# Value and query projections first, gate projections last, within each block of a fused retention and mixture-of-experts kernel

## What is computed

```python
xn = layernorm(x)                                  # no scale, no shift
q, v = xn @ Wq, xn @ Wv
states = scan(lambda prev, vt: lam * prev + vt, v) # along the tokens
y = q * states
y = (y - mean(y)) * rsqrt(var(y) + 1e-5) * ln_g + ln_b   # over 1024 features
attn = (y * silu(xn @ Wg)) @ Wo
# router: top 8 of 64 experts for a token, at most 128 tokens an expert
h  = silu(xg @ w1[e].T) * (xg @ v1[e].T)           # 384 wide
ffn = scatter_add(weight * (h @ w2[e]))
out = x + attn + ffn
```

## Time and profile before

| | |
|---|---|
| time, median of 3 runs | 2774.52 us (2772.79 to 2777.97) |
| the profiled execution: time / span | 2767.81 us / 2766.1 us |
| PE busy | 2572.7 us, 93% |
| DVE busy | 1640.1 us, 59% |
| ACT busy | 1295.2 us, 47% |
| POOL busy | 633.0 us, 23% |
| mean granted TensorE clock | 0.967 of full |

### The profile page before, as it was taken

One profiled execution on the slowest core, in us unless ns is written; L12 is line 12 of the kernel. 1 busy time (PEld: TensorE's weight loads), 2 busy tenths in 40 slices (PEclk: granted clock), 3 DMA queues, 4 the chain that ended last, 5 costly groups with the idle time before them and its releaser, 6 DMA issues.

```text
span 2766.1 us, 41220 instructions
## 1 busy us (share of the span) xinstructions
PE 2572.7 (93%) x13849; PEld 2280.4 (82%) x13849; DVE 1640.1 (59%) x1718; ACT 1295.2 (47%) x1474; POOL 633.0 (23%) x521
## 2 busy tenths in 40 slices
PE   4799699999999899998999989999899998999997
PEld 4787588879888798887988889888898888988786
DVE  7868745466545655547655575545755457554664
ACT  5533234445544455444644455444554445544454
POOL 1001212132221412113221241221321214221321
PEclk8899899999999999999999999999999999999998
DMA  7646375658855587656875569756686567956576
GB/s 279 220 151 212 122 231 162 223 171 257 263 189 191 183 270 236 212 172 201 273 253 188 175 208 296 233 162 209 221 264 227 180 204 221 294 174 213 184 246 162
DMA packets 147556, 590.16 MB, mean 213 GB/s; under 512 B 20096, under 2 KB 36544, under 8 KB 147008
## 3 DMA queue, kind: packets, MB, share of 16 engines
q1 hardware_dynamic: 112128, 503.71, 50.7%
q0 software_dynamic: 35392, 86.00, 15.5%
HBM read 520.89 MB, written 85.50 MB: 219 GB/s over the span
## 4 chain that ended last, share of the span: by engine, by line
PE 68%; DMA 12%; issue 9%; DVE 6%; ACT 3%; POOL 2%; POOLq 0%; ACTq 0%; DVEq 0%
PE psA L1165 15%; PE psA L1167 15%; PE psA L1166 14%; DMA out_dram<-ot 7%; DMA out_dram<-ys,s_idx 5%; PE psH L1165 5%; PE psH L1167 4%; PE psH L1166 4%; PE psY L1165 2%; PE psY L1167 2%; PE psY L1166 2%; DVE yb L960 2%; ACT ew_hi L632 1%; PE psX L1269 1%; DVE ew_lo L913 1%
## 5 line engine op out<-in xcount | busy, mean ns | idle before, releaser
L913 DVE TENSOR_TENSOR ew_lo<-ew_raw,ew_hi 128x1536 fp32r<-128x1536 f32 x377 | 667.3, 1778 | 395.5 <-ACT ew_hi L632 389.9
L632 ACT ACTIVATE ew_hi<-ew_raw 128x1536 fp32r<-128x1536 f32 x384 | 567.2, 1487 | 176.2 <-DMA ew_raw<-ew_dram 104.2
L1165 PE MATMUL psA<-xT_hi,pw_hi 128*128 128x512 f32 x1536 | 616.9, 402 | 2.0 <-DVE pw_lo L908 2.0
L1167 PE MATMUL psA<-xT_hi,pw_lo 128*128 128x512 f32 x1536 | 608.6, 396 | 0.0
L1166 PE MATMUL psA<-xT_lo,pw_hi 128*128 128x512 f32 x1536 | 604.2, 393 | 0.0
L626 ACT ACTIVATE pw_hi<-pw_raw 128x1024 fp32r<-128x1024 f32 x256 | 267.8, 1061 | 515.9 <-PE psA L1167 515.9
L908 DVE TENSOR_TENSOR pw_lo<-pw_raw,pw_hi 128x1024 fp32r<-128x1024 f32 x256 | 309.0, 1218 | 257.6 <-ACT pw_hi L626 252.2
L1165 PE MATMUL psH<-ew_hi,gT_hi 128*128 128x384 f32 x1024 | 360.3, 352 | 37.5 <-DVE gT_lo L934 37.5
L1166 PE MATMUL psH<-ew_lo,gT_hi 128*128 128x384 f32 x1024 | 354.2, 346 | 0.0
L1167 PE MATMUL psH<-ew_hi,gT_lo 128*128 128x384 f32 x1024 | 353.8, 346 | 0.0
L1167 PEld LDWEIGHTS psA<-xT_hi,pw_lo 128*128 128x128 f32 x1536 | 290.8, 189 | 69.9
(11 more groups left out here) (152 smaller groups left out, 3318.8 us busy)
## 6 DMA issues: line engine op xcount, KB each, us to landing
ew_raw<-ew_dram SPq DMA_DIRECT2D x384, 768.0 KB, 5.7
pw_raw<-proj_w_dram SPq DMA_DIRECT2D x256, 512.0 KB, 3.6
xn_scratch<-xt SPq DMA_DIRECT2D x33, 512.0 KB, 3.8
xt<-x_dram SPq DMA_DIRECT2D x32, 512.0 KB, 5.9
out_dram<-x_dram SPq DMA_DIRECT2D x32, 512.0 KB, 5.0
out_dram<-ot POOLq DMA_DIRECT2D x32, 512.0 KB, 13.6
xn<-xn_scratch SPq DMA_DIRECT2D x29, 512.0 KB, 6.2
xn_scratch<-wt SPq DMA_DIRECT2D x33, 32.0 KB, 1.5
```

The source lines that it names most:

```text
L632: act.activation(ew_hi[:, c % 3, :], ew_raw[:, c % 3, :], ACT.Copy).then_inc(s_ewhi, 1)
L913: dve.tensor_tensor(ew_lo[:, c % 3, :], ew_raw[:, c % 3, :], ew_hi[:, c % 3, :].bitcast(F32), ALU.subtract).then_inc(s_ewlo, 1)
L1165: pe.matmul(dst, l_hi, r_hi_, start=first, stop=False)
L1167: return pe.matmul(dst, l_lo, r_hi_, start=False, stop=last)
```

## The change

The order of the projections in a block changes. The loop becomes `vq`: four steps with four projections each (v, q, v, q). The eight gate projections follow it, straight in the code, and the part between is laid under them. `Wg` moves behind `Wv`, `Wq` in the table of weights, and the loads follow the new order. The number of matmuls is the same.

v always goes to bank 0 of `psA` and q to bank 1. Token sums and their transpose move to `psH`, the shifts to `psY`. The shift (now `shift_in`) and the gating (`gate_in`) go chunk by chunk, with a semaphore `s_t` of their own; a shift matmul waits until the shift two before has been added. POOL no longer makes the low part of expert piece 1. Its gather in the loop moves ahead of the second `add_sums`. In block 0 the 16 rounds are 3 a step and then 4 under the gates.

```diff
@@ vector engine, loop @@
                     scan(j, mm, 0)
                     S(2)
-                    find(0)
+                    next8(0)
                     times_q(j, mm, 0)
                     S(3)
-                    strike(0)
                     if with_e:
                         hT_lo_of(e)
                         piece_lo(e + 1, 0)
+                    next8(1)
+                    scan(j, mm, 1)
+                    if with_e:
+                        piece_lo(e + 1, 1)
+                        gT_lo_of(e + 1)
+                        piece_lo(e + 1, 2)
                     S(4)
-                    if with_e:
-                        piece_lo(e + 1, 1)
-                        piece_lo(e + 1, 2)
-                        gT_lo_of(e + 1)
-                    find(1)
-                    strike(1)
-                    scan(j, mm, 1)
+                    times_q(j, mm, 1)
                     S(5)
-                    find(2)
-                    times_q(j, mm, 1)
-                    S(6)
-                    strike(2)
-                    S(7)
-                    find(3)
-                    strike(3)
+                    next8(2)
                     if with_e:
                         hidden_part(e + 1)
@@ vector engine, under the gates @@
+                for m in range(2, KC):
+                    G(m + 2)
+                    if not with_e and m < 6:
+                        find8(keys[:, :], l1, 10 + m, s_ext, s_l1)
+                        strike8(keys[:, :], 10 + m, s_ext)
+                    if m == 2:
+                        shift_in(j, 0)
+                    shift_in(j, m - 1)
+                    if m == 2:
+                        gate_in(j, 0)
+                    if m == KC - 1:
+                        shift_in(j, m)
+                    gate_in(j, m - 1)
+                gate_in(j, KC - 1)
                 if with_e:
                     piece_lo(e + 1, 3)
-                z_of(j, 3)
@@ gpsimd @@
+                def vq(mm):
                     add_sums(j, mm, 0)
                     if with_e:
                         scatter(e0 + mm, 4 * j)
+                        gather_next(e0 + mm + 1)
                     add_sums(j, mm, 1)
-                    if with_e:
-                        gather_next(e0 + mm + 1)
...
-                    if with_e and m == 1:
-                        scatter(e0 + 4, 4 * j)
-                        gather_next(e0 + 5)
@@ scalar engine, under the gates @@
+                for m in range(2, KC):
+                    G(m + 2)
+                    gate(j, m)
+                    if m == 2:
+                        z_hi_of(j, 0)
+                    z_hi_of(j, m - 1)
                 if with_e:
                     piece_hi(e + 1, 3)
-                z_his(j, 2)
-                z_his(j, 3)
+                z_hi_of(j, KC - 1)
@@ tensor engine @@
-                token_sums(j)
+                g_proj(j, 0)
+                if with_e:
+                    hidden_turn(e)
+                token_sums(j)
+                g_proj(j, 1)
+                if with_e:
+                    output_mm(e)
+                    gather_turn(e + 1)
                 token_turn(j)
-                if with_e:
-                    gather_turn(e + 1)
-                shifts(j, 0)
-                if with_e:
-                    output_mm(e, (1,))
-                for i in range(1, 4):
-                    shifts(j, i)
-                    if with_e:
-                        hidden_mm(e + 1, (i - 1,))
-                if with_e:
-                    hidden_mm(e + 1, (3,))
+                g_proj(j, 2)
+                pe.wait_ge(s_t6, j + 1)
+                if with_e:
+                    pe.wait_ge(s_ys, e + 1)
+                shift(j, 0)
+                for m in range(3, KC):
+                    shift(j, m - 2)
+                    g_proj(j, m)
+                shift(j, KC - 2)
+                if with_e:
+                    hidden_mm(e + 1, (0,))
+                shift(j, KC - 1)
+                if with_e:
+                    hidden_mm(e + 1, (1, 2, 3))
```

More of the change, by code:

```diff
@@ L405, in run @@
                 with_e = e0 is not None
-                def qvg(mm):
+                def vq(mm):
                     per = NTOK // P // (KC // 2)
-                    for a in range(2, 8):
-                        if with_e and a == 6:
+                    for a in range(2, 6):
+                        if with_e and a == 4:
                             load_rest(e0 + mm + 1)
-                        load_proj(a % 2, 6 * mm + a + 2, n1(j, mm, a) + 1)
+                        load_proj(a % 2, 4 * mm + a + 2, n1(j, mm, a) + 1)
                         if not with_e:
-                            for i in range((a - 2) * per // 6, (a - 1) * per // 6):
+                            for i in range((a - 2) * per // 4, (a - 1) * per // 4):
                                 copy_x(per * mm + i)
@@ L417, in qvg @@
                         load_first(e0 + mm + 2)
-                each_qvg(sp, qvg)
+                each_vq(sp, vq)
+                for m in range(2, KC + 2):
+                    if with_e and m == 4:
+                        load_rest(e0 + 5)
+                    load_proj(m % 2, 2 * KC + m + 2, ng(j, m) + 1)
                 if with_e:
-                    load_rest(e0 + 5)
                     load_first(e0 + 6)
@@ L525, in run @@
                 if with_e:
[L526 to L530, removed]
+                    scatter(e0 + 4, 4 * j)
+                    gather_next(e0 + 5)
                 for m in range(KC - 1):
@@ L1065, in qvg @@
[L1065 to L1069 removed]
+                    S(4)
+                    times_q(j, mm, 1)
+                    S(5)
+                    next8(2)
                     if with_e:
                         hidden_part(e + 1)
[L1073 removed]
+                each_vq(dve, vq)
+                G = lambda m: proj_lo(ng(j, m), m % 2)
+                e = None if not with_e else e0 + 4
@@ L1098, in run @@
                 if with_e:
-                    hidden(e + 1)
                     piece_lo(e + 1, 4)
                     piece_lo(e + 1, 5)
-                if not with_e:
+                    hidden(e + 1)
+                else:
+                    dve.wait_ge(s_l1, SLOTS // 8)
+                    dve.tensor_copy(l2[:, 0:SLOTS], l1[0:SEL, :]).then_inc(s_lf, 1)
                     dve.wait_ge(s_l2, 16)
@@ L1317, in token_turn, with shift @@
                 for t in range(NT):
-                    o = pe.transpose(psA[:, 1, t * P:(t + 1) * P], tok6[:, t, :], ident[:, :])
+                    o = pe.transpose(psH[:, 1, t * P:(t + 1) * P], tok6[:, t, :], ident[:, :])
                 o.then_inc(s_tT, 1)
-            def shifts(j, i):
-                if i == 0:
-                    pe.wait_ge(s_t6, j + 1)
-                for m in (2 * i, 2 * i + 1):
-                    if i > 0:
-                        pe.wait_ge(s_z, 2 * KC * j + 4 * i - 3 + m % 2)
-                    pe.matmul(psA[:, m % 2, :], ln6T[:, m, :], tok6T[:, :], start=True, stop=True
-                              ).then_inc(s_sh, 1)
+            def shift(j, m):
+                if m > 1:
+                    pe.wait_ge(s_t, KC * j + m - 1)
+                pe.matmul(psY[:, m % 2, :], ln6T[:, m, :], tok6T[:, :], start=True, stop=True
+                          ).then_inc(s_sh, 1)
             def run(j, e0, last):
```

161 lines of the change are left out of this document (75 added, 86 removed).

## The result

The changed kernel takes 2685.55 us (median of 4 runs, 2678.09 to 2686.97); in the same session the kernel before took 2774.73 us (2772.79 to 2777.97). The ratio is 0.9672, 95% interval 0.9651 to 0.9693: 89 us faster, where 72 were predicted. The profiled execution took 2684.2 us with a span of 2682.5 us; the mean granted clock rose from 0.967 to 0.981.

The account below looks back on a forecast made before the run. TensorE was taken to bound the loop, with a chain on other engines bare between loop and `out_proj`. Gates' part -83, lock +11, block 0 0: -72 on 2767.8 gives 2696, median 6.7 above: 2702 us; 8-in-10 range 2678 to 2740.

Parts of the forecast that it names:

- the own case: Whole kernel: faster by 50 to 90 us, 2684 to 2724; chance 0.64.
- rival (c): Neither loss comes: VectorE gets in first in the loop (11), piece 3 is in time (11): 2680; chance 0.12.
- The cover: Blocks 1 to 7: work of the part between hides under gate projections of 5.63 us each, no stall up to gate 7.
- the bare end: Behind gate 7, blocks 1 to 7: TensorE waits 1.6 us ahead of expert piece 3, for its `ew_lo`.
- the lock: Loop, blocks 1 to 7: GpSimd's second sums hold VectorE's `ew_lo`; TensorE waits 0.4 us a step, 11 us in all.
- block 0's rounds: Block 0: `find8`/`strike8` rounds of 5.14 us on VectorE delay TensorE, in the loop and under the gates.
- The gates' part: Blocks 1 to 7: a stretch costs 20.1 us instead of 31.43; 11.8 a block with 0.5 for clock, 83 for seven.
- DMA and SP: Loop, blocks 1 to 7: DMA's mean rises from 200 to 233 GB/s, SP meets the same waits; priced at nothing.
- rival (d): Slower: the lock hits every step fully, VectorE waits 2.5 us, a step loses 4, 112 us in all: 2803; chance 0.05.
- The head of `out_proj`: Start of `out_proj`, blocks 1 to 7: no longer at the low clock, 0.5 us gained a block.
- `outp`: Third stage of a block: nothing in its scatter chain changes, zero; a head start could give 0 to 7 us.
- Block 0: Block 0: loop loses some 2 us, 26 lost afterwards against 25.44 and 2 before; taken as 0, from -5 to +5.

Follow-up runs that it names:

- piece 3 first: Against the changed kernel, under gate 7 ScalarE rounds piece 3 before `z_hi` 6 and VectorE splits it before the last gatings: 2673.92 us.
- sums later: Against the changed kernel, GpSimd's second pair of sums in a step waits until VectorE has made `ew_lo` of piece 3: 2681.1 us.
- four more: Against the changed kernel, four more GpSimd additions into an unread tile follow the second pair of sums in every step with an expert: 2693.32 us.
- rounds behind the gatings: Against the changed kernel, block 0's four rounds under the gates stand behind each gating instead of ahead of the shift: 2680.07 us.
- four more that round: Against the changed kernel, four GpSimd subtractions writing a rounded, unread tile follow the second pair of sums in every step with an expert: 2688.5 us.
- z bare: Against the changed kernel, shifts, gatings and splits of z stand behind all gates again, in pairs, token sums staying under the gates: 2731.32 us.

## Why the prediction was right, and by how much it missed

The forecast of 2702 rested on the own case, faster by 50 to 90; measured are 89, at that case's edge. The measured 2685.55 is nearer to rival (c)'s 2680 than to my 2702, so the time alone wouldn't tell the two apart. The rows do: both losses that (c) denies, in the loop and ahead of piece 3, are there. The cover, the bare end, the lock and block 0's rounds are all in the trace where the working put them. By its steps:

- **The gates' part.** Loop and part between, the lock's wait taken out, were forecast at 190.19 + 20.1 = 210.3 a block; 211.0 - 1.2 = 209.8 was measured. No stall up to gate 7, as argued. The single wait ahead of piece 3 was forecast at 1.6, measured at 1.6, on the path that was named (split of Wo's weights, shifts 6 and 7, gating 6, `z_hi` 6, `ew_hi`, `ew_lo`); *piece 3 first* removes exactly it. DMA and SP were priced at nothing: in block 2's first part, at 229 GB/s where 233 was forecast for the loop, TensorE is busy 152.37 of 152.49 us. The base of 31.43 varies by itself: the repeated profile of before has 31.84 for the same parts.
- **The lock in the loop.** Forecast 0.4 a step, measured 0.30, 8.4 us instead of 11; *sums later* takes 8.7 out. The rule of the Trainium skill that was cited with it ("SBUF — State Buffer", section "Who interferes with whom": the one issued first holds the ports for its whole length) agrees with the held `ew_lo` of that row and with each single hold in *four more*. It doesn't cover the row of 7.42, of which the prediction said that it agrees; the last section has that row. Rival (c)'s premise, that VectorE gets in first, is not what happens; rival (d)'s, a wait of 2.5 us on VectorE, would need two instructions of GpSimd ahead of one of VectorE's, and in the loops of these kernels it waited for the running one alone.
- **The head of `out_proj`.** I took 0.5 a block for its clock. By the starts of its first 48 matmuls it lost 0.56 to 1.60 before, 5.96 us over seven blocks, and 0.03 each after. 5.8 us instead of 3.5.
- **`outp`.** Forecast zero, with 0 to 7 as a bound. Six stages went from 676.6 to 669.4 us and the last block's third part from 132.24 to 128.99: 10.5 less, of which 5.8 is the head above. The other 4.7, 0.7 a block, are not explained. Single stages vary (110.3 to 114.3 in the traces of changed kernels, 111.2 to 114.8 in those of the kernel before), but not all of it is spread: the seven third parts sum to 808.9 and 808.8 us in the two traces of before, and to 796.7 to 802.8 in the ten of changed kernels with z under the gates, 799.7 in the mean. Some 9 us are gained, then, about 3 of them for a reason that no run shows.
- **Block 0.** Forecast 0 from -5 to +5; measured -3.4 (244.13 to 240.76 from its loop's start to block 1's). The waits are where they were named, for `pw_lo` and `yb` behind the rounds; *rounds behind the gatings* removes 8 us. But that the sum is near 0 is in part luck, since two terms missed in opposite directions. Loop and gate 0 took 104.48 us, 8.8 more than 17 projections of 5.63, where the old loop lost 5.2: 3.6 worse, not 2. The stretch to `out_proj` took 59.94, 20.5 beyond its seven projections, where I had put 26. Together they give -1.3, which repeats; the other 2 are block 0's `outp`, 76.3 here and 77.4 to 80.3 in all other traces.
- **The part ahead.** It took 4.6 us more in the trace after than in the trace of before, with unchanged code; the repeated profile of before shows that as spread.

The sum of the spans then reads: -74.4 for loops and gates' parts (forecast -68.3), -10.5 for `outp` (forecast -3.5), -3.4 block 0 (0), +4.6 ahead: -83.6 before rounding, the spans' difference. What is left to the 89 of the medians is the profiled execution of before, which lay 6.9 us under its median, and that of after, 1.4 under. I added the distance of before to the forecast and so took it that the changed kernel would have the same. Against the repeated profile of before (2774.5) the spans differ by 92, and loops and gates' parts by 77.2 instead of 74.4.

So the mechanism was right, and every mis-sized term but the part ahead erred to the same side, too little gain. They are `outp` with the head of `out_proj` (7.0 us), the stretch itself (3.5), block 0 (3.4), the lock (2.6), and 5.3 that two profiles lie differently to their medians, less the 4.6 ahead: 17 us.

## What to carry to other kernels

Lay a chain of short steps on other engines under the long matmuls that don't depend on it, piece by piece, and count for each engine what it must do within one such matmul group. Then look at the end, where the cover stops: there the order in the queues of ScalarE and VectorE decides, and whatever TensorE needs first should be first in them, ahead of work that is needed only later. A second small order of the same kind, which of two engines touches SBUF first, was worth 9 us here because it repeated 28 times.

## What the runs showed of the hardware

VectorE and GpSimd, both reading SBUF, took turns. In rows of three and six GpSimd instructions a waiting `ew_lo` (lengthened by 0.83 to 0.93 us) got in as soon as the running one ended, and then held GpSimd's next (2.55 instead of 1.29). The kernel before shows the same in block 2: the pair of gatings of 3.60 stands beside two `z_lo` that are lengthened as well. And where VectorE's instruction was first, GpSimd's was the held one (`ew_lo` in its 1.76 us, `y_sum` 2.25):

```profile
947.82 3.42 POOL L533 TENSOR_TENSOR z_lo<-yb,z_hi 128x512 fp32r<-128x512 f32 x2
...
756.30 1.76 DVE L913 TENSOR_TENSOR ew_lo<-ew_raw,ew_hi 128x1536 fp32r<-128x1536 f32 x1
...
756.97 2.25 POOL L503 TENSOR_TENSOR y_sum<-y_sum,yb 128x512 f32<-128x512 f32 x1 [12.62 <-ACT sq L669]
```

Yet in the same kernel one gating waited about 6.1 us, through five `z_lo` of 1.23 each. The pair with it took 7.42 to 7.47 in blocks 2 to 7, and none of the five `z_lo` was lengthened. In block 1 a gating waited about 5.5 us through four:

```profile
623.19 6.79 DVE L960 TENSOR_TENSOR yb<-yb,gb 128x512 f32<-128x512 f32 x2
...
623.87 4.95 POOL L533 TENSOR_TENSOR z_lo<-yb,z_hi 128x512 fp32r<-128x512 f32 x4
```

The first of the two gatings takes 6.19 of the 6.79. By their starts the gating was the earlier one, by 0.09 us in blocks 2 to 7 (958.95 against 959.03) and by 0.68 in block 1, and still it was the one that waited, and for the whole row. The form of GpSimd's instruction doesn't explain it (*four more that round*), nor do gatings as such (*z bare*, where they took turns). What sets these rows apart was not tried. It stays open.
